# A graph network's prologue: y split on two engines beside the table chain, item tables sent first

## The chip, the cores and the metric

One NeuronCore of one Trainium2 chip runs the whole program in one launch. The metric is the device time of an execution in microseconds (us). The engines are named as in the profile: PE is TensorE (PEld its weight loads), DVE is VectorE, ACT is ScalarE, POOL is GpSimd, SP is SyncE; a letter q behind a name (SPq, DVEq) is that engine's instruction queue.

## The reference

The graph has 6250 nodes and 100000 edges, sorted by destination (dst), with features of 128 floats. Two blocks follow one another.

```python
def _sage_layer(x, src, dst, Wl_i, bl_i, Wr_i):
    agg = segment_sum(x[src], dst, N_NODES)
    cnt = segment_sum(ones, dst, N_NODES)
    return agg / clip(cnt, 1.0)[:, None] @ Wl_i + bl_i + x @ Wr_i      # three layers, relu after the first two
x = layernorm(x + sage(x))
z = concatenate([x[dst], x[src], edge_attr])                            # the convolution
msg = sigmoid(z @ Wf.T + bf) * softplus(z @ Ws.T + bs)
agg = batchnorm(segment_sum(msg, dst, N_NODES))
x = layernorm(x + relu(layernorm(agg + x)) + x)
```

## The kernel before, in words

**Data.** Nodes are cut into 49 windows of 128 rows (NW), windows into 7 chunks of 7 (NCH, CW); edges into 784 tiles of 128 (NT). A layer first makes y = h @ Wl and keeps it in DRAM (`y_dram`), and the residual h @ Wr in SBUF (`res`). For layer 0 these are `first_y` (L780) and `first_res` (L790) on PE, `first_copy` (L1198) and `first_res_copy` (L1204) on ACT. SP stores y chunk by chunk (L453).

**Two ways of summing.** 256 tiles (KT) whose destinations span fewer than 12 rows are summed densely: DVE builds two one-hots for a tile (`build`, L1909), PE multiplies them to counts (`count`, L895), ACT evicts them (`evict`, L1261), and for each of 26 groups of 10 tiles PE multiplies the counts with y (`multiply`, L914, 49 matmuls). For this product y stands in SBUF split into three bf16 parts (`y_parts`), whose sum is y to float accuracy: cast to bf16, subtract, cast the rest, subtract, cast. The other 528 tiles are gathered: POOL fetches 128 rows of y for each with an indirect DMA (L724), four tiles are a quad, 132 quads in a layer, in a ring of 12 (RQ). An item is a product of a quad with one window's one-hot: DVE builds the one-hot (`onehots`, L1898), PE multiplies (`item`, L905), DVE adds to `acc` (`add_item`, L1958). 182 items a layer make 26 turns of 7 (IT); 17 of them are woven with the counting, the last 9 with the adding of dense groups by pairs. SP feeds POOL: it sends the indices of a quad into `idx` when the slot's last item has been summed (`quad`, L532), ten quads ahead (AHEAD).

**Tables.** Which quad, window and column an item has is computed on the chip. DVE works out the schedule in a long chain of small instructions, from L1659 on: tiles are ranked and permuted (perms, L1686, with PE's products L831 to L841), then `schedule` and `part_of` make the item tables (to L1799), and a second call of `schedule` (L1800) the convolution's. PE transposes them (L861, L868), DVE copies them out (L1828, L1832), SP carries them through DRAM into one row of SBUF, `q_regs` and `regs` (L499 to L508). The engines read them there with `reg_load`: 7 words at an address of `it * 7` for each turn's list on PE (L887, L888) and DVE (L1906, L1954), and 12 on SP (L521).

**Order around the change.** All of it is written out by hand, with semaphores between the engines. DVE waits for `order_ready`, which SP raises at L493 after all stores of y have landed, before it starts the chain. ACT copies all seven residual chunks, waits for `q_regs` (L1208), then reads y back from DRAM two chunks at a time (`read_y`, L1241). DVE clears `acc` (L1835), waits for both tables (L1836), writes constants (L1839), and starts on the layer (`sage_adds`, L2040). Layer 0's first pair of turns is `counting_turns(0, first=True)`: before the additions of items 0 to 4 it splits chunks 0; 1, 2; 3, 4; 5; 6 (`SPLITS_AT`, `split_y`, L1927). In layers 1 and 2 the same split is done in their first turns.

```python
SPLITS_AT = [[0], [1, 2], [3, 4], [5], [6]]
...
                        if first and at < len(SPLITS_AT):
                            for c in SPLITS_AT[at]:
                                split_y(0, c)
                        add_item(0, it, i, sums, columns)
```

Of the kernel before, what the change touches and what calls it, by code (L numbers as in the profile page):

```python
# [5 lines left out]
P = 128  # L6
N = 6250
E = 100000
F = 128
# [12 lines left out]
CW = 7  # L22
# [29 lines left out]
NIC = 2  # L52
OH_SLOTS = [0, 1, 2, 3, 0, 1, 2]
# [18 lines left out]
SPLITS_AT = [[0], [1, 2], [3, 4], [5], [6]]  # L72
# [11 lines left out]
assert NW == CW * NCH and EP == P * NT  # L84


def build_gnn(nc, x, xT, src, dst, srcT, ea, eaT, w0, bl, blT, w1, we, b1, bn, out):
# [11 lines left out]
    with ctx:  # L99
# [20 lines left out]
        regs_dram = dram("regs_dram", (3 * NC, P), i32)  # L120
        q_regs_dram = dram("q_regs_dram", (6 * NIC, P), i32)
# [18 lines left out]
        q_regs = sb("q_regs", [1, 6 * NIC * P], i32)  # L140
# [46 lines left out]
        y_again = [work[:, EA_AT + k * CW * F:EA_AT + (k + 1) * CW * F].rearrange("p (u f) -> p u f", f=F) for k in range(2)]  # L187
        iota_c = dlo[:, 0:CELLS // 2].bitcast(bf16)
# [115 lines left out]
        tabT = work[0:3 * NC, 9344:9344 + P].bitcast(i32)  # L304
        q_tabT = work[0:6 * NIC, 9472:9472 + P].bitcast(i32)
# [13 lines left out]
        tabf = sb("tabf", [P, 3, NC])  # L319
        q_tabf = sb("q_tabf", [P, 6, NIC])  # L320
# [20 lines left out]
        def ps_first(h):  # L341
# [15 lines left out]
            chosen permuted y_in y_split cells counted counts_put multiplied reduced dense_sent nat_in order_ready idx_given ea_sorted rows rowsf rows_tr dlo_ready  # L357
# [51 lines left out]
        P_BANKS = (0, 1, 6, 7)  # L409

# [22 lines left out]
        def _(sp):  # L433
# [67 lines left out]
            sp.dma_start(q_regs[:, :], q_regs_dram.rearrange("r p -> (r p)").rearrange("(o k) -> o k", o=1))\  # L501
                .then_inc(s["tab_back"], 16)
            sp.wait_ge(s["tabT"], 2)
            sp.wait_ge(s["tab_back"], 32)
            sp.dma_start(regs_dram, tabT).then_inc(s["tab_back"], 16)
            sp.wait_ge(s["tab_back"], 48)
            sp.dma_start(regs[:, :], regs_dram.rearrange("r p -> (r p)").rearrange("(o k) -> o k", o=1))\
# [12 lines left out]
            def load_items(first, a, b):  # L520
                sp.reg_load(l_regs[a:b], q_regs[0:1, bass.ds(first, b - a)])  # L521
# [8 lines left out]
            def sage_quads(layer):  # L530

                def quad(it, q, done):  # L532
                    ahead = q + AHEAD
                    if isinstance(it, int) and it * RQ + ahead >= QG:
# [10 lines left out]
                def turn(it):  # L545
                    n = RQ if not isinstance(it, int) or it == 0 else RQ - AHEAD
                    first = it * RQ + (4 * NIC * P + AHEAD - RQ)
                    if isinstance(it, int) and it == 0:
                        done = [None] * (RQ - AHEAD) + load_items(4 * NIC * P, RQ - AHEAD, RQ)
                    else:  # L550
                        done = load_items(first, 0, n) + [None] * (RQ - n)
# [29 lines left out]
            with sp.Fori(0, NCH) as it:  # L581
# [3 lines left out]
                sp.wait_ge(s["x1_sent"], (it + 1) * 16)  # L585
# [7 lines left out]
            sp.wait_ge(s["tab_back"], 64)  # L593
            sp.wait_ge(s["tab_back"], 32)
# [37 lines left out]
            def needed(m):  # L632
                sp.reg_load(n_regs, q_regs[0:1, bass.ds(m * RC + (5 * NIC * P - RC), RC)])
# [136 lines left out]
        def _(pe):  # L770
# [51 lines left out]
            te.matmul(ps[0:ROWS, 7, 8:9], lhsT=tri[0:ROWS, 0:ROWS], rhs=t_cum[:, CH - 1:CH], start=True, stop=True).then_inc(s["permuted"], 1)  # L822

# [20 lines left out]
            first_res(0)  # L844
# [16 lines left out]
            te.transpose(ps[0:6 * NIC, 5, 0:P], q_tabf[:, :, :].rearrange("p r c -> p (r c)"), ident[:, :])\  # L861
                .then_inc(s["tables_put"], 1)
            for c in range(NIC):
# [4 lines left out]
            te.transpose(ps[0:3 * NC, 5, P:2 * P], tabf[:, :, :].rearrange("p r c -> p (r c)"), ident[:, :])\  # L868
                .then_inc(s["tables_put"], 1)
            pe.wait_ge(s["loads"], LOADS * 16)  # L870
            pe.wait_ge(s["ones_col"], 2)
            pe.wait_ge(s["tab_back"], 32)
# [6 lines left out]
            def sage_sums(layer):  # L879
# [6 lines left out]
                def load_turn(it):  # L886
                    pe.reg_load(t_regs, q_regs[0:1, bass.ds(it * IT, IT)])  # L887
# [1503 lines left out]
```

## Time and profile before

| | |
|---|---|
| three runs | 3545.97, 3549.5, 3554.33 us; median 3549.5 |
| the profiled execution | 3549.38 us, span 3547.6 us |
| busy, share of the span | PE 75%, DVE 61%, ACT 34%, POOL 65% |
| granted TensorE clock over the span | 0.895 of full |
| layer 0, first and last addition of an item (L1962) | 126.1 us and 869.5 us |
| first and last gather of layer 0 (L724) | 63.56 us and 863.33 us |

The busy shares are means over the whole program. The change touches the first 190 us, so the rows below are mostly of that stretch. In a list of instructions the brackets at the end of a row hold the idle time of its engine ahead of it and what ended it. The granted clock is a share of 2.4 GHz.

### The profile page before, as it was taken

Reading aid. Unit: us, or ns where it says so; the run is one execution under the profiler, and the core shown is the slowest. Engines: PE = TensorE matmul, PEld = TensorE weight load, DVE = VectorE, ACT = ScalarE, POOL = GpSimd, SP = SyncE. Lnnn points to the kernel's source line nnn. Section 1 sums busy time; section 2 is a strip of 40 time slices with the busy share of each in tenths; the row PEclk is TensorE's granted clock in tenths of the full one; section 3 lists DMA queues with packets and bytes.
Section 4 is the critical chain, followed back from the end, with each engine's and each line's share of the span. In section 5 each row is a group of like instructions: output and inputs, shape, how many; then the busy total and the mean of one; then the engine's idle time right before and its main releaser. Section 6 shows DMA issues by size and latency. Waiting matters only on the chain. (4 is left out here: it accounts for less than half of the span.)

```text
span 3547.6 us, 70629 instructions
## 1 busy us (share of the span) xinstructions
PE 2659.6 (75%) x16221; PEld 1996.7 (56%) x16222; DVE 2168.2 (61%) x4954; ACT 1192.1 (34%) x1646; POOL 2317.7 (65%) x2399
## 2 busy tenths in 40 slices
PE   5368888666697776566888765578888888888874
PEld 5145555465465555464555554556666666666653
DVE  5834544355732224457554544568888888888886
ACT  1023332200100000010000000158888888888865
POOL 2357777576677777756777777537777777777620
PEclk8589999887799998777989987899999999999997
DMA  4254444322565553226877752254444444444421
GB/s 122 77 169 145 139 131 143 112 50 59 153 172 156 146 149 97 53 66 184 245 222 241 221 137 63 56 159 126 127 127 126 128 126 127 126 116 119 114 58 37
DMA packets 345773, 454.44 MB, mean 128 GB/s; under 512 B 135431, under 2 KB 260386, under 8 KB 342099
## 3 DMA queue, kind: packets, MB, share of 16 engines
q0 software_dynamic: 88624, 207.58, 21.7%
q10 hardware_dynamic: 101984, 181.27, 15.9%
q1 hardware_dynamic: 155092, 64.77, 7.0%
q8 instruction: 27, 0.44, 0.1%
q14 instruction: 46, 0.38, 0.0%
HBM read 357.03 MB, written 101.90 MB: 129 GB/s over the span
## 5 line engine op out<-in xcount | busy, mean ns | idle before, releaser
L724 POOL DMA_INDIRECT shared<-y_dram,idx x1584 | 1523.1, 962 | 681.2 <-issue 506.4
L910 PE MATMUL ps<-shared,work 128*128 x4368 | 680.7, 306 | 384.3 <-issue 220.6
L764 POOL DMA_INDIRECT shared<-q_dram,idx x784 | 777.5, 992 | 284.0 <-issue 204.6
L910 PEld LDWEIGHTS ps<-shared,work 128*128 128x128 f32 x4368 | 619.5, 216 | 452.4 <-issue 440.2
L1962 DVE TENSOR_TENSOR acc<-acc,ps 128x129 f32 x546 | 156.4, 286 | 891.7 <-PE ps L910 736.6
L1114 PE MATMUL ps<-pq,work 128*128 x1664 | 497.0, 401 | 150.3 <-issue 87.6
L2251 DVE TENSOR_TENSOR work<-ps,shared 128x256 f32<-128x256 f32 x832 | 294.8, 416 | 175.6 <-PE ps L1117 156.4
L1114 PEld LDWEIGHTS ps<-pq,work 128*128 128x128 f32 x1664 | 256.6, 195 | 244.5 <-issue 173.4
L929 PE MATMUL ps<-pq,work 128*128 128x385 bf16 x1456 | 296.2, 354 | 84.4 <-DVE work L1950 34.4
L1386 ACT ACTIVATE pq<-ps,blT_sb 128x512 f32<-128x512 f32 (+1 forms) x28 | 16.5, 632 | 888.2 <-PE ps L1013 888.2
L1265 ACT CAST work<-ps 128x600 bf16<-128x600 f32 x260 | 159.8, 661 | 413.3 <-PE ps L902 344.9
L1900 DVE SCALAR_TENSOR_TENSOR work<-ps,w_of,dstT_sb 128x512 f32<-128x512 f32 x370 | 275.2, 745 | 1.2 <-issue 1.2
L1467 ACT ACTIVATE work<-work 128x1024 f32<-128x1024 f32 x208 | 219.8, 1057 | 125.8 <-DVE work L2251 125.7
L929 PEld LDWEIGHTS ps<-pq,work 128*128 128x128 bf16 x1456 | 149.9, 104 | 186.5 <-issue 79.7
L2260 DVE SCALAR_TENSOR_TENSOR work<-work,ps 128x1024 f32<-128x1024 f32 x208 | 251.5, 1209 | 1.3 <-ACT ps L1477 1.3
L1133 PE MATMUL ps<-work 128*128 128x128 f32 x1664 | 242.0, 289 | 0.8 <-DVE work L2272 0.8
L1409 ACT ACTIVATE rs<-ve 128x7 f32<-128x7 f32 x21 | 4.4, 210 | 691.6 <-DVE ve L2165 691.0
L1117 PE MATMUL ps<-we_rows,ea_sb 128*128 128x256 bf16 x832 | 230.4, 277 | 0.0
L1133 PEld LDWEIGHTS ps<-work 128*128 128x128 f32 x1664 | 202.2, 192 | 48.2 <-issue 48.2
L1473 ACT ACTIVATE work<-work 128x1024 f32<-128x1024 f32 x208 | 216.6, 1041 | 0.0
L1477 ACT ACTIVATE ps<-work 128x1024 f32<-128x1024 f32 x208 | 213.9, 1028 | 6.6
L929 PE MATMUL ps<-shared,work 128*128 128x385 bf16 x1092 | 204.3, 336 | 2.3 <-DVE shared L1933 2.3
(359 smaller groups left out, 3627.8 us busy)
## 6 DMA issues: line engine op xcount, KB each, us to landing
work<-counts_dram ACTq DMA_DIRECT2D x156, 384.0 KB
counts_dram<-work ACTq DMA_DIRECT2D x26, 1568.0 KB
shared<-y_dram,idx POOLq DMA_INDIRECT x1584
ea_parts<-work ACTq DMA_DIRECT2D x128, 196.0 KB
ea_sb<-ea_parts SPq DMA_DIRECT2D x196, 128.0 KB
work<-counts_dram ACTq DMA_DIRECT2D x52, 416.0 KB
shared<-q_dram,idx POOLq DMA_INDIRECT x784
y_dram<-work SPq DMA_DIRECT2D x21, 448.0 KB, 3.1
```

Of the source, the lines that this page charges most:

```text
L724: pool.indirect_dma_start(msg[:, u, 0:F], None, y_dram, bass.IndirectOffsetOnAxis(ap=idx[:, u:u + 1], axis=0)).then_inc(s_quad[q], 16)
L764: pool.indirect_dma_start(q_ring[:, u * 2 * F:(u + 1) * 2 * F], None, q_dram, bass.IndirectOffsetOnAxis(ap=idx[:, u:u + 1], axis=0)).then_ ...
L910: last = te.matmul(ps[:, SUM_BANKS[i], 0:FA], lhsT=oh4[:, OH_SLOTS[i], u, :], rhs=shared[:, bass.ds(place + u * FA, FA)], start=u == 0, st ...
L929: last = te.matmul(ps[:, DENSE_BANK, 0:YB - 1], lhsT=counts[:, w, :], rhs=y_parts(w, 1)[:, 0, 0:YB - 1], start=w == 0, stop=w == NW - 1)
L1114: te.matmul(o, lhsT=ohT[:, (slot - 1) % 2, t, :], rhs=pq[:, bass.ds(w_of_pair[t] * (2 * F), 2 * F)], start=True, stop=False)
L1117: last = te.matmul(o, lhsT=ea_sb[:, bass.ds(e_of_pair[t] * P, P)], rhs=we_rows[:, :], start=False, stop=True)
L1133: te.matmul(ps_flat[:, bass.ds(blocks[t] * P + AGG_BANK * 512, P)], lhsT=oh[:, (slot - 3) % GB, t, :], rhs=mm[:, (slot - 3) % 2, t, :], st ...
L1467: sc.activation(log_, pre[:, slot % 2, :, :], ACT.Abs).then_inc(s["absd"], 1)
L1473: sc.activation(log_, log_, ACT.Exp, scale=-1.0).then_inc(s["expd"], 1)
L1900: v.scalar_tensor_tensor(out=oh4[:, slot, :, :], in0=(iota_ps if layer else iota[:, :]).unsqueeze(1).to_broadcast([P, QT, P]), scalar=w_of ...
L2251: last = v.tensor_tensor(pre[:, slot % 2, t, :], ps_pre[:, slot % 2, t, :], q_ring[:, bass.ds(slots[t] * (2 * F), 2 * F)], ALU.add)
L2260: v.scalar_tensor_tensor(out=gates, in0=pre_, scalar=0.0, in1=ps_log, op0=ALU.max, op1=ALU.add)\
```

## The change

1. DVE's chain waits for the loads of dst and src (`nat_in`) itself; `order_ready` is gone.
2. PE does the residual products 0 to 2 right after its first triangular product, ahead of the permutations; ACT copies these three, then reads y.
3. Y is split with ACT and DVE together. ACT reads four chunks at once into four buffers (`y_first`), casts, DVE subtracts (`less_part`), twice; then chunks 4 to 6. ACT's queue is: four reads, four casts, residual copies 3 to 6, the clearing of `acc`, four second casts, four third casts with the next three reads between them, nine casts. DVE subtracts chunks 0 to 3 between the item tables and the convolution's schedule, chunks 4 to 6 after it, and then waits for `y_split` to reach 7.
4. The item tables are signalled, transposed and copied out before the convolution's schedule is computed. One of their six rows, the convolution's, moves to the other table.
5. `q_regs` is laid out anew: each turn's seven words stand in eight, written by eight DMAs; a read of seven words becomes one of four and one of three, each at a multiple of four; SP's of twelve become three of four. This holds for all layers.
6. SP sends 12 quads of indices up front instead of 10.

```diff
+Q_TABLES = [(NEEDED_AT, 0, 0, TURNS, IT, WIDE), (PLACES_AT, 1, 0, TURNS_ALL, IT, WIDE), ...
+y_first = [work[:, at_:at_ + CW * F]... for at_ in (EA_AT, EA_AT + CW * F, 6328, 6328 + CW * F)]
 # SP
-            sp.sem_inc(s["order_ready"], 1)
-            for q in range(AHEAD):
+            for q in range(RQ):
                 sp.dma_start(idx[:, q * QT:(q + 1) * QT], src_c[:, q * QT:(q + 1) * QT]).then_inc(s_idx[q], 16)
-            sp.dma_start(q_regs[:, :], q_regs_dram...)
+            for at_, row_, first_, turns_, n_, wide_ in Q_TABLES:
+                sp.dma_start(q_regs[0:1, at_:at_ + turns_ * wide_]..., from_dram).then_inc(s["tab_back"], 16)
 # PE
             te.matmul(ps[0:ROWS, 7, 8:9], lhsT=tri[0:ROWS, 0:ROWS], ...).then_inc(s["permuted"], 1)
+            for it in range(3):
+                first_res(it)
...
-            first_res(0)
...
-            first_res(1)
-            for it in range(2, NCH):
+            for it in range(3, NCH):
                 first_res(it)
...
                 def load_turn(it):
-                    pe.reg_load(t_regs, q_regs[0:1, bass.ds(it * IT, IT)])
-                    pe.reg_load(g_regs, q_regs[0:1, bass.ds(it * IT + NIC * P, IT)])
+                    for k in range(0, IT, 4):
+                        pe.reg_load(t_regs[k:k + 4], q_regs[0:1, bass.ds(it * WIDE + (NEEDED_AT + k), min(4, IT - k))])
+                        pe.reg_load(g_regs[k:k + 4], q_regs[0:1, bass.ds(it * WIDE + (PLACES_AT + k), min(4, IT - k))])
 # ACT
-            for it in range(NCH):
+            for it in range(3):
                 first_res_copy(it)
-            act.wait_ge(s["tab_back"], 32)
+            def read_first(c):
+                act.dma_start(y_first[c % 4], y_dram[...]).then_inc(s[Y_FIRST[c % 4]], 16)
+            def cast_first(c, k):
+                if k == 0:
+                    act.wait_ge(s[Y_FIRST[c % 4]], (c // 4 + 1) * 16)
+                else:
+                    act.wait_ge(s["y_made"], subs_before(c, k))
+                sc.copy(y_parts(c * CW, CW)[:, :, k * F:(k + 1) * F], y_first[c % 4]).then_inc(s["y_cast"] if k < 2 else s["y_split"], 1)
+            act.wait_ge(s["permuted"], 4)
+            for it in (NCH - 2, NCH - 1):
+                act.wait_ge(s[Y_SENT[it % 2]], (it // 2 + 1) * 16)
+            for c in range(4):
+                read_first(c)
+            for c in range(4):
+                cast_first(c, 0)
+            for it in range(3, NCH):
+                first_res_copy(it)
+            sc.copy(acc[:, :], zero[:, :].to_broadcast([P, NW * FA])).then_inc(s["acc_clear"], 1)
+            for c in range(4):
+                cast_first(c, 1)
+            act.wait_ge(s["permuted"], 7)
+            for c in range(4):
+                cast_first(c, 2)
+                if c + 4 < NCH:
+                    act.wait_ge(s["y_split"], c + 1)
+                    read_first(c + 4)
+            for k in range(3):
+                for c in range(4, NCH):
+                    cast_first(c, k)
+            act.wait_ge(s["tab_back"], TAB_Q)
 # DVE
-            dve.wait_ge(s["order_ready"], 1)
+            dve.wait_ge(s["nat_in"], 32)
...
+            alone(dve)
+            dve.sem_inc(s["tab"], 1)
+            dve.wait_ge(s["tables_put"], 2)
+            v.tensor_copy(q_tabT, ps[0:5 * NIC, 5, 0:P]).then_inc(s["tabT"], 1)
+            dve.wait_ge(s["tables_put"], 3)
+            link(v.tensor_copy(w_of[:, :], ps[:, 6, 0:NIC * P]))
+            def less_part(c, k):
+                dve.wait_ge(s["y_cast"], casts_before(c, k))
+                v.tensor_tensor(y_first[c % 4], y_first[c % 4], y_parts(c * CW, CW)[:, :, k * F:(k + 1) * F], ALU.subtract).then_inc(s["y_made"], 1)
+            for k in range(2):
+                for c in range(4):
+                    less_part(c, k)
             schedule(7, NC, kcol, S_)
...
-            dve.wait_ge(s["r0"], NCH)
-            v.memset(acc[:, :], 0.0).then_inc(s["acc_clear"], 1)
-            dve.wait_ge(s["tab_back"], 64)
+            for k in range(2):
+                for c in range(4, NCH):
+                    less_part(c, k)
+            dve.wait_ge(s["y_split"], NCH)
+            dve.wait_ge(s["tab_back"], TAB_Q + 16)
...
-                        if first and at < len(SPLITS_AT):
-                            for c in SPLITS_AT[at]:
-                                split_y(0, c)
                         add_item(0, it, i, sums, columns)
```

## Rows read from the trace of the kernel before

**Rows 1.** Stretches: length, busy us of each engine, granted clock, DMA share, GB/s
```profile
120.00:166.00 46.00, 11.82 (x54) 8.81 (x53) 45.04 (x63) 6.10 (x10) 3.96 (x4) 0.54 0.28 92
189.00:411.00 222.00, 181.67 (x1145) 118.56 (x1143) 99.88 (x329) 65.16 (x106) 154.75 (x160) 0.93 0.50 161
411.00:671.00 260.00, 228.78 (x1443) 150.65 (x1444) 127.63 (x422) 83.62 (x136) 183.15 (x188) 0.96 0.44 138
```

**Rows 2.** Groups of DVE, 113 to 166.2 us: busy us, mean ns | idle before
```profile
L1933 DVE CAST pq<-work 128x896 bf16<-128x896 f32 x12 | 12.9, 1079 | 0.3
L1933 DVE CAST shared<-work 128x896 bf16<-128x896 f32 x9 | 9.8, 1084 | 0.2
L1936 DVE TENSOR_TENSOR work<-work,pq 128x896 f32<-128x896 f32 x8 | 8.7, 1092 | 0.3
L1936 DVE TENSOR_TENSOR work<-work,shared 128x896 f32<-128x896 f32 x6 | 6.5, 1092 | 0.2
```

**Rows 3.** Waits, 125 to 190 us: us in total, times, longest
```profile
POOL shared L724 <- DMA idx<-ea_sb: 64.4, 1, 64.4
```

**Rows 4.** Instructions in time, all engines: start us, us, what, idle before
```profile
51.54 5.85 PE L831 MATMUL ps<-pq,shared 112*128 112x264 f32 x16 [6.58 <-DVE pq L1688]
...
60.99 6.39 SPq L496 DMA_DIRECT2D idx<-ea_sb  x10
...
69.59 2.83 PE L841 MATMUL ps<-work,shared 112*128 112x264 f32 x12
...
102.86 1.06 PE L864 MATMUL ps<-work,ones 128*128 128x128 f32 x4
...
123.95 0.94 POOL L724 DMA_INDIRECT shared<-y_dram,idx  x1 [0.30 <-issue]
...
186.82 21.63 SPq L540 DMA_DIRECT2D idx<-ea_sb  x6
...
189.26 0.94 POOL L724 DMA_INDIRECT shared<-y_dram,idx  x1 [64.38 <-DMA idx<-ea_sb]
```

**Rows 5.** Instructions of DVE in time
```profile
26.57 0.21 DVE L1595 COPY work<-ps 128x50 f32<-128x50 f32 x1 [1.98 <-PE ps L804]
...
39.24 0.63 DVE L1659 CAST shared<-shared 112x896 f32<-112x896 int32 x1 [12.47 <-SPq L492]
...
95.89 0.48 DVE L1799 TENSOR_SCALAR work<-ident,work 128x128 f32<-128x128 f32 x2
...
105.01 0.17 DVE L1824 COPY conv_w<-work 128x7 f32<-128x7 f32 x1
...
113.37 0.21 DVE L1839 TENSOR_SCALAR dlo<-iota 128x44 bf16<-128x44 f32 x1 [0.16 <-DMA regs<-regs_dram]
...
186.87 0.29 DVE L1962 TENSOR_TENSOR acc<-acc,ps 128x129 f32 x1 [1.60 <-PE ps L910]
...
294.53 0.29 DVE L1962 TENSOR_TENSOR acc<-acc,ps 128x129 f32 x1 [2.23 <-PE ps L910]
...
319.35 0.29 DVE L1962 TENSOR_TENSOR acc<-acc,ps 128x129 f32 x1 [0.23 <-PE ps L910]
```

**Rows 6.** DMA issues, 0 to 70 us: KB each, median us to landing
```profile
shared<-in_src SPq DMA_DIRECT2D x1, 392.0 KB, 10.0
```

**Rows 7.** Table reads by line (ns min/median/max; last row: 114 to 115 us)
```profile
L887 PEldq TENSOR_LOAD <-q_regs x78: 1061/1702/2653, 109.3 to 2252.8; - x78
L1906 DVEq TENSOR_LOAD <-q_regs x84: 528/1626/3966, 114.5 to 2255.3; - x84
L1859 DVEq TENSOR_LOAD <-regs x208: 337/342/357, 2353.3 to 3425.2; - x104
L1906 DVEq TENSOR_LOAD <-q_regs x1: 768/768/768, 114.5 to 114.5; - x1
```

**Rows 8.** Groups of ACT: busy us, mean ns | idle before
```profile
L1206 ACT COPY pq<-ps 128x896 f32<-128x896 f32 x7 | 6.3, 906 | 49.6 <-PE ps L797 49.6
```

**Rows 9.** DMA issues, 108 to 120 us
```profile
work<-y_dram ACTq DMA_DIRECT2D x2, 448.0 KB, 4.1
```

More of the change, by code:

```diff
@@ L52 @@
 NIC = 2
+WIDE = 8
 OH_SLOTS = [0, 1, 2, 3, 0, 1, 2]
@@ L71 @@
 COUNTS_LAST = [2, 3, 3, 2, 4, 3, 3]
-SPLITS_AT = [[0], [1, 2], [3, 4], [5], [6]]
 FIRST_SLOTS = 6
@@ L187, in build_gnn @@
         y_again = [work[:, EA_AT + k * CW * F:EA_AT + (k + 1) * CW * F].rearrange("p (u f) -> p u f", f=F) for k in range(2)]
+        y_first = [work[:, at_:at_ + CW * F].rearrange("p (u f) -> p u f", f=F) for at_ in (EA_AT, EA_AT + CW * F, 6328, 6328 + CW * F)]
         iota_c = dlo[:, 0:CELLS // 2].bitcast(bf16)
@@ L520, in load_items @@
             def load_items(first, a, b):
-                sp.reg_load(l_regs[a:b], q_regs[0:1, bass.ds(first, b - a)])
+                for k in range(a - a % 4, b, 4):
+                    lo, hi = max(a, k), min(b, k + 4)
+                    sp.reg_load(l_regs[lo:hi], q_regs[0:1, bass.ds(first + lo, hi - lo)])
                 for q in range(a, b):
@@ L533, in quad @@
                     ahead = q + AHEAD
-                    if isinstance(it, int) and it * RQ + ahead >= QG:
+                    if isinstance(it, int) and (it * RQ + ahead >= QG or layer == 0 and it == 0 and ahead < RQ):
                         pass
@@ L632, in needed @@
             def needed(m):
-                sp.reg_load(n_regs, q_regs[0:1, bass.ds(m * RC + (5 * NIC * P - RC), RC)])
+                for k in range(0, RC, 4):
+                    sp.reg_load(n_regs[k:k + 4], q_regs[0:1, bass.ds(m * WIDE + (CONV_DONE_AT - WIDE + k), min(4, RC - k))])
                 for q in range(RC):
@@ L933, in load_pairs @@
                 def load_pairs(turn):
-                    pe.reg_load(d_regs, q_regs[0:1, bass.ds(turn * IT + (NIC * P + NI1), IT)])
+                    for k in range(0, IT, 4):
+                        pe.reg_load(d_regs[k:k + 4], q_regs[0:1, bass.ds(turn * WIDE + (PLACES_AT + TURNS * WIDE + k), min(4, IT - k))])
                     return [pe.snap(r, min_val=0, max_val=(NGR - PT) * FA) for r in d_regs]
@@ L1248, in read_y @@
                         .then_inc(s["y_in"], 16)
-                for it in (NCH - 2, NCH - 1):
-                    act.wait_ge(s[Y_SENT[it % 2]], (it // 2 + 1) * 16 if layer == 0 else y_sent(layer - 1, it))
-                if layer == 0:
-                    act.wait_ge(s["permuted"], 4)
-                elif layer == 1:
-                    act.wait_ge(s["rowsf"], 1)
-                for c in range(2):
-                    read_y(c)
-                if layer == 0:
-                    act.wait_ge(s["y_split"], 1)
+                if layer:
+                    for it in (NCH - 2, NCH - 1):
+                        act.wait_ge(s[Y_SENT[it % 2]], y_sent(layer - 1, it))
+                    if layer == 1:
+                        act.wait_ge(s["rowsf"], 1)
+                    for c in range(2):
+                        read_y(c)
                 def evict(n, k, row):
@@ L1905, in load_columns @@
             def load_columns(first, n):
-                dve.reg_load(c_regs[0:n], q_regs[0:1, bass.ds(first, n)])
+                for k in range(0, n, 4):
+                    dve.reg_load(c_regs[k:min(k + 4, n)], q_regs[0:1, bass.ds(first + k, min(4, n - k))])
                 return [dve.snap(r, min_val=0, max_val=(QL - 1) * QT) for r in c_regs[0:n]]
@@ L1927, in split_y @@
             def split_y(layer, c):
-                dve.wait_ge(s["y_in"], (layer * NCH + c + 1) * 16)
-                if c == 0 and not layer:
-                    v.memset(counts[:, :, GT * SPAN:P], 0.0)
+                dve.wait_ge(s["y_in"], Y_IN0 + ((layer - 1) * NCH + c + 1) * 16)
                 y_, p_ = y_again[c % 2], y_parts(c * CW, CW)
@@ L1980, in load_pairs @@
             def load_pairs(turn):
-                dve.reg_load(b_regs, q_regs[0:1, bass.ds(turn * IT + (3 * NIC * P + NI1), IT)])
-                dve.reg_load(f_regs, q_regs[0:1, bass.ds(turn * IT + (2 * NIC * P + NI1 + LOOK), IT)])
+                for k in range(0, IT, 4):
+                    dve.reg_load(b_regs[k:k + 4], q_regs[0:1, bass.ds(turn * WIDE + (SUMS_AT + TURNS * WIDE + k), min(4, IT - k))])
+                    dve.reg_load(f_regs[k:k + 4], q_regs[0:1, bass.ds(turn * WIDE + (PAIR_COLS_AT + k), min(4, IT - k))])
                 return ([dve.snap(r, min_val=0, max_val=(NW - 1) * FA) for r in b_regs],
```

112 lines of the change are left out of this document (69 added, 43 removed).

## The prediction

> **What bounds the kernel now.** The page's first section comes first: PE, DVE and GpSimd (POOL) are each busy for well over half of the span and none for nearly all of it. The shares name no single bound, so the stage that the change touches is read alone. Next the stretches: from 120 to 166 us DVE works 45.04 of 46 us while PE has 11.82 and POOL 3.96; from 189 us on it is the other way round, PE 181.67 of 222 us, POOL 154.75, DVE 99.88 [rows 1]. DVE bounds 46 us and little afterwards. The groups of that stretch say what it does: 21 casts and 14 subtractions of 128x896, the split of y into three bf16 parts, 12.9 + 9.8 + 8.7 + 6.5 = 37.9 us [rows 2]. They stand between the first additions of items. The waits say who pays: POOL has one wait of 64.4 us for an index transfer [rows 3], from the gather at 123.95 to the one at 189.26. SyncE issues that transfer only at 186.82 [rows 4], since its slot is free only when enough items have been summed, and items are summed as fast as DVE takes them. The eighth addition is at 186.87 [rows 5]. Everything after hangs on it: a gather starts 1.25 us after the one before (0.94 and 0.30 of issue, [rows 4]), so the layer's other 480 gathers alone are 600 us, and the counting that PE does beside them starts there too. I carry the sum out for the moment of the eighth addition.
>
> **1. The order is not awaited behind y's stores.** DVE ends L1595 at 26.78 and starts L1659 at 39.24, a wait of 12.47 us for SyncE's L492 [rows 5]. What L1659 needs are dst and src in rows; src is issued third on SyncE's queue, in the first 5 us, and landed 10.0 us later [rows 6], by 15. The gain is between 0 (reading the flag and jumping over the fallback costs DVE as much as the wait did) and 12.5. For the flag and the jump, which the wait covered, I leave 2.2 us: an estimate between one and two table reads of 0.77 to 1.63 [rows 7]. So 10.2. PE's last y product ends at about 32, DVE's first step comes at about 34, and three residual products behind it, under 2 us each with ACT's 0.906 copies between them [rows 8], end near 40 (an estimate), before the permutations come at 51.54 - 10.2 = 41.3 [rows 4]. The permutation matmuls began at the lower rate (16 in 5.85 us, 0.366 each; of the later, same-shaped ones 12 in 2.83, 0.236 [rows 4]); with PE busy just before them up to 2 us could come back. I count nothing.
>
> **2. The item tables ahead of the convolution's.** DVE ends L1799 at 96.37 [rows 5]; shifted 86.2, and 0.3 for two chained writes: signal at 86.5. PE's transpose and the four passes of L864 take until about 1.5 us after the signal (end 103.92 [rows 4]); two copies more, 88.6. SyncE then issues eight small transfers where it had one. Ten index transfers took 6.39 us to issue [rows 4]; eight such are over before 96, with nothing queued behind them but the convolution's tables, which DVE finishes at 106; PE waits for them, but has no item before DVE's one-hots. So they cost nothing, and up to 5 us if that cover went.
>
> **3. The split beside the chain.** ACT may read y once the last permutation matmul is over, 72.42 [rows 4] - 10.2 = 62.2. A 448 KB read took 4.1 us [rows 9]; four one after another land by 79 at worst. ACT's copy of 896 columns costs 0.906 [rows 8]: the four first casts are done at 80, the four residual copies at 85.5 (in step with PE's products, and before 86.5, when PE is wanted for the tables), and the clearing of acc, 6321 columns at the same rate, at 92. For ACT's casts out of SBUF, which no row shows, the bounds are 0.9 [rows 8] and twice that; I take 1.0, beside DVE's 1.08 [rows 2]. DVE subtracts chunks 0 to 3 twice, 8 x 1.09 [rows 2] = 8.7 us, 88.6 to 97.4, with ACT one chunk behind it. The convolution's schedule took from 96.3 to 105.2 [rows 5], 8.9 us: 106.3. A transpose and a copy, 1.1: 107.4. ACT's third casts and the reads of chunks 4 to 6 start near 97 and land by 109.5; three casts, six subtractions (6.5 us) and the last two casts end at 116. Fourteen subtractions remain on DVE, the 21 casts and the clear do not.
>
> So DVE begins the constants of L1839 at 116 instead of 113.37 [rows 5], 2.6 us late: it has swapped a wait and a clear for 15.2 us of subtractions. What is gone is what came after. Before, the builds ahead of item 0 were over at 120.5, just where the first cast began; now at 123.5 with a memset. From there on there are only builds and additions: seven items and one dense product took 294.53 to 319.35, 24.8 us [rows 5]. The clock granted was 0.54 from 120 to 166, nearly the lower of the levels 1.2 and 2.4 GHz, with PE mostly idle, and 0.93 from 189 to 411 [rows 1]; the new turn begins low, and as in L831 some 16 matmuls pay, 16 x (0.366 - 0.236) = 2 us. Eighth addition: 123.5 + 24.8 + 2 = 150, against 186.87: **37 us**.
>
> The index transfer and POOL's restart follow it as before, 152 for 189. The first 48 gathers also start and end 10 us earlier, worth nothing; so are the two index transfers that SyncE sends up front in addition (12 for 10), on an idle queue.
>
> **4. Table reads in fours.** Each read of seven words becomes one of four and one of three. Seven words took 1.63 (DVE) and 1.70 us (PE) in the median and 1.06 at PE's lowest, three words 0.768, four aligned words in the convolution 0.342 [rows 7]. The lows come when the start is a multiple of four, every fourth turn: four words travel together there, the rest singly. So the new pair costs 0.34 + 0.77 + 0.1 of address = 1.2 us; three turns in four it gains 0.4 to 0.5, in the fourth it loses 0.15. PE has two reads a turn, 17 turns in layer 0's counting part: at most 10 us if PE were the bound throughout. From 189 to 411 POOL is nearly always at work (154.75 busy of 222, where 0.94 of 1.25 would be 167); from 411 to 671 it gives way (183.15 of a possible 195) and PE has 228.78 of 260 [rows 1]. Nine turns, two reads, 0.25: 4; I take 2. In layers 1 and 2 POOL's gathers bound: 0. Both ends: 10 gained, 3 lost (an instruction more for each read and none faster).
>
> The Trainium skill speaks against this part: "Runtime: NRT & Kernel Launch", section "Instruction fetch mechanics", gives such a load some 200 ns for each register, even in bulk. By that rule seven words cost the same whole or split, the term is 0, and the sum 3512. The seven-word median agrees (0.23 a word); the four words in 0.342 do not.
>
> **Sum.** The profiled execution took 3549.38 us, its span 3547.6. 3549.4 - 37 - 2 = **3510**. The three runs' median is 3549.5 (3545.97 to 3554.33), so it holds for that too.
>
> **Rivals.**
> (a) *The start is late or cold.* If ACT's casts out of SBUF cost double, DVE is ready some 8 us later, and if PE stays at the lower rate for the whole first turn, its 24.8 us grow by up to half. For it: 0.54 granted there [rows 1]. Against: the rate rose within one group of matmuls in L831. Time 3520 to 3530.
> (b) *More than the sum.* The full 12.5 us of part 1, 2 of the permutations, 8 more of the table reads: 3498 to 3501. For it: PE at 0.88 of 411 to 671 [rows 1]. Against: POOL's ring caps it.
> (c) *The gathers take it back.* If POOL's own stream ended layer 0 from its first gather on, only that gather's start would count, and a stop between layers could swallow the 10 us: 3540 to 3549. Against: the 64.4 us [rows 3] are a hole in that very stream, and it closes with the eighth item.
> (d) *Slower: y's reads choke the table chain.* ACT takes reads, casts and residual copies in order; the copies free PE for the item tables, which DVE awaits. Seven reads of r us move the start by about 7 (r - 4.1). From r = 9.4 on the kernel loses; at three times the row, 12.3, it takes 3510 + 57 = 3567. For it: four reads stand at once beside the gathers, which is new. Against: the two of the row ran beside gathers too, at 4.1 [rows 9].
>
> **How the numbers follow.** No change can be told from one within 0.2%, 7 us. Chances: forecast (3502 to 3519) 0.66, (a) 0.15, (b) 0.10, (c) 0.05, of which most is within 0.2%, (d) 0.04. The range goes down to (b)'s 3498 and up to (a)'s 3530; (c), (d) and the tails of (a) and (b) are left out, some 0.15. Faster 0.92, same 0.04, slower 0.04.
>
> **What would show it.** The chain of L1659 starts near 29, with no wait of 12 us. The subtractions stand in two groups, near 89 to 97 without gaps and near 108 to 115. The constants of L1839 come at 114 to 118. DVE has no cast of 128x896 in layer 0. The eighth item is added near 150, and POOL's longest wait for an index in layer 0 is near 40 us (112 to 152), not 64. Three-word reads take 0.77 and four-word reads 0.34. The layer's last addition moves as much as the eighth. I am wrong if the eighth item comes early and the last does not, or if ACT's residual copies behind the reads end after 87 and hold the tables up.

## The result, and the profile after

The changed kernel takes 3501.2 us (median of 4 runs, 3492.5 to 3502.4) where the kernel before took 3548.6: ratio 0.9859, 95% interval 0.9845 to 0.9872, 47 us less by the medians and 50 by the ratio. The profiled execution spans 3500.4 us against 3547.6. The forecast was 3510 in a range of 3498 to 3530.

The marks of layer 0, the first additions after and before (L2037 is L1962 of before): eighth item, item 113 (the first of turn 16), last of the layer.

DVE in time, after; columns: start us, us, engine line op out<-in, count, [idle before <- what ended it]:
```profile
148.85 0.29 DVE L2037 TENSOR_TENSOR acc<-acc,ps 128x129 f32 x1 [1.54 <-PE ps L946]
...
592.02 0.29 DVE L2037 TENSOR_TENSOR acc<-acc,ps 128x129 f32 x1 [2.54 <-PE ps L946]
...
823.36 0.29 DVE L2037 TENSOR_TENSOR acc<-acc,ps 128x129 f32 x1 [6.19 <-PE ps L946]
```
The same two later marks before:
```profile
640.64 0.29 DVE L1962 TENSOR_TENSOR acc<-acc,ps 128x129 f32 x1 [1.74 <-PE ps L910]
...
869.48 0.29 DVE L1962 TENSOR_TENSOR acc<-acc,ps 128x129 f32 x1 [4.35 <-PE ps L910]
```
The eighth addition moved from 186.87 [rows 5] to 148.85, by 38.0 us. From there to turn 16 (I call it the woven stage: 15 turns with counting) it was 453.8 us and is 443.2, 10.6 less. The last nine turns give 2.5 back (228.8 to 231.3). At the layer's end the gain is 46.1, at the ends of layers 1 and 2 it is 48.8 and 49.2: some 3 more are won in the two together.

The stretches of after that answer to [rows 1], each begun at nearly the same work:
```profile
118.00:152.00 34.00, 27.68 (x168) 20.47 (x169) 20.30 (x66) 11.80 (x20) 7.26 (x8) 0.83 0.17 62
152.00:374.00 222.00, 183.24 (x1157) 118.18 (x1156) 102.63 (x340) 66.54 (x109) 158.41 (x162) 0.95 0.50 162
374.00:622.00 248.00, 222.02 (x1417) 142.97 (x1417) 123.77 (x409) 81.25 (x133) 182.61 (x187) 0.99 0.45 144
```
The stretch in which DVE worked 45 of 46 us is gone: in its place PE works 27.7 of 34 us at a granted clock of 0.83 where it had 0.54. The last stretch does nearly the same matmuls and gathers (1417 and 187, before 1443 and 188) in 248 us instead of 260.

The chain of DVE, after (compare [rows 5]):
```profile
26.42 0.21 DVE L1661 COPY work<-ps 128x50 f32<-128x50 f32 x1 [1.99 <-PE ps L840]
32.18 0.63 DVE L1726 CAST shared<-shared 112x896 f32<-112x896 int32 x1 [5.55 <-issue]
32.72 0.62 DVE L1727 TENSOR_SCALAR shared<-shared 112x896 int32<-112x896 int32 x1
34.89 0.63 DVE L1728 TENSOR_SCALAR shared<-shared 112x896 int32<-112x896 int32 x1 [1.54 <-issue]
...
91.31 8.10 DVE L1876 TENSOR_TENSOR work<-work,pq 128x896 f32<-128x896 f32 x8
...
107.95 0.17 DVE L1903 COPY conv_w<-work 128x7 f32<-128x7 f32 x1
108.78 0.28 DVE L1907 CAST work<-ps 23x128 int32<-23x128 f32 x1 [0.66 <-PE ps L904]
108.98 6.08 DVE L1876 TENSOR_TENSOR work<-work,shared 128x896 f32<-128x896 f32 x6
116.07 0.19 DVE L1914 TENSOR_SCALAR dlo<-iota 128x44 bf16<-128x44 f32 x1 [1.00 <-ACT shared L1259]
```
The wait of 12.47 us for SyncE has gone, and a stop of 5.55 us that no other engine ends has come, with a second of 1.54. The subtractions stand in two groups, one before and one behind the convolution's schedule, and the constants (L1839 before, L1914 now) begin at 116.07, released by ACT's last cast.

ACT beside it:
```profile
65.27 3.26 ACTq L1251 DMA_DIRECT2D work<-y_dram  x4
69.09 0.94 ACT L1259 CAST pq<-work 128x896 bf16<-128x896 f32 x1 [21.46 <-DMA work<-y_dram]
70.80 0.94 ACT L1259 CAST pq<-work 128x896 bf16<-128x896 f32 x1 [0.77 <-DMA work<-y_dram]
...
82.91 0.91 ACT L1243 COPY pq<-ps 128x896 f32<-128x896 f32 x1 [0.66 <-PE ps L833]
83.71 5.46 ACT L1271 COPY acc<-zero 128x6321 f32<-128x6321 f32 x1
```
POOL's restart, 64.38 us of wait before [rows 4]:
```profile
151.33 1.40 POOL L760 DMA_INDIRECT shared<-y_dram,idx  x1 [24.91 <-DMA idx<-ea_sb]
```
The wait is shorter by more than the start moved, since the first 48 gathers start 7.1 us earlier (56.46 for 63.56) but end 1.5 later (126.42 for 124.89).

The table reads (ns, least/median/most), four-word and three-word ones together on a line:
```profile
L923 PEldq TENSOR_LOAD <-q_regs x156: 333/700/978, 108.9 to 2204.4; - x156
L1982 DVEq TENSOR_LOAD <-q_regs x162: 344/742/2329, 117.4 to 2205.5; - x162
```

### The profile page after: what moved, and what is told of

The parts are those of the page before. It is cut to its first block, busy times and chain, and to the rows that moved or that the text cites. A ratio compares the mean times of both kernels' runs of the same rounds, so it can differ in the third digit from the quotient of the medians.

```text
span 3500.4 us, 71571 instructions
## 1 busy us (share of the span) xinstructions
PE 2665.2 (76%) x16221; PEld 2000.1 (57%) x16222; DVE 2142.4 (61%) x4932; ACT 1216.7 (35%) x1668; POOL 2333.4 (67%) x2399
## 4 chain that ended last, share of the span: by engine, by line
POOL 35%; PE 21%; issue 19%; DVE 10%; DMA 9%; DVEq 3%; SPq 2%; ACT 2%; POOLq 0%; ACTq 0%
POOL shared L760 28%; POOL shared L800 8%; DMA shared<-q_dram,idx 6%; PE ps L955 6%; PE ps L946 4%; PE ps L1151 3%; PE ps L938 2%; SPq L638 1%; DVE work L2326 1%; PE ps L965 1%; DVE work L2010 1%; PE ps L1154 1%; DMA counts_dram<-work 1%; DVE work L2335 1%; ACT work L1481 1%
## 5 line engine op out<-in xcount | busy, mean ns | idle before, releaser
L760 POOL DMA_INDIRECT shared<-y_dram,idx x1584 | 1538.5, 971 | 623.3 <-issue 498.9
L2037 DVE TENSOR_TENSOR acc<-acc,ps 128x129 f32 x546 | 156.3, 286 | 901.8 <-PE ps L946 770.9
L2326 DVE TENSOR_TENSOR work<-ps,shared 128x256 f32<-128x256 f32 x832 | 294.6, 416 | 177.6 <-PE ps L1154 149.4
L1452 ACT ACTIVATE pq<-ps,blT_sb 128x512 f32<-128x512 f32 (+1 forms) x28 | 16.5, 631 | 887.6 <-PE ps L1050 887.6
```

The lines of the kernel that those rows point to most:

```text
L760: pool.indirect_dma_start(msg[:, u, 0:F], None, y_dram, bass.IndirectOffsetOnAxis(ap=idx[:, u:u + 1], axis=0)).then_inc(s_quad[q], 16)
L2326: last = v.tensor_tensor(pre[:, slot % 2, t, :], ps_pre[:, slot % 2, t, :], q_ring[:, bass.ds(slots[t] * (2 * F), 2 * F)], ALU.add)
```

## The experiments

"Stage" is the time from the eighth addition to turn 16. The marks are of the profiled execution, the total is the median of all; the ratio is to the kernel before, run beside it on the same chip. Its medians there were 3548.6 to 3553.2, so two totals of this table compare to a few us only.

| kernel | eighth | stage | layer 0 ends | total | ratio, 95% interval | name |
|---|---|---|---|---|---|---|
| before | 186.9 | 453.8 | 869.5 | 3548.6 | 1 | |
| after | 148.9 | 443.2 | 823.4 | 3501.2 | 0.9859 (0.9845 to 0.9872) | |
| before + reads | 190.0 | 442.0 | 862.9 | 3539.8 | 0.9972 (0.9962 to 0.9981) | e1 |
| after, reads whole | 150.2 | 451.4 | 832.7 | 3511.1 | 0.9897 (0.9882 to 0.9912) | e2 |
| before + order | 182.0 | 454.0 | 865.6 | 3544.2 | 0.9989 (0.9980 to 0.9998) | e3 |
| after, order awaited | 153.9 | 445.3 | 830.5 | 3503.3 | 0.9872 (0.9857 to 0.9887) | e4 |
| split only (and PE's products ahead) | 153.3 | 451.4 | 836.3 | 3519.7 | 0.9916 (0.9899 to 0.9932) | e5 |
| after, tables late | 148.8 | 444.1 | 824.1 | 3500.1 | 0.9865 (0.9848 to 0.9881) | e6 |
| after again (PE) | 149.5 | 444.1 | 825.9 | 3500.0 | 0.9857 (0.9840 to 0.9873) | e10 |
| after again (DVE) | 148.0 | 443.6 | 823.4 | 3502.8 | 0.9868 (0.9852 to 0.9885) | e11 |
| after, PE's reads slow | 149.2 | 459.7 | 840.0 | 3521.4 | 0.9911 (0.9898 to 0.9925) | e12 |
| after, DVE's reads slow | 149.4 | 455.3 | 835.4 | 3509.3 | 0.9872 (0.9857 to 0.9887) | e13 |
| after, reads of eight | 147.3 | 419.4 | 795.3 | 3470.6 | 0.9772 (0.9759 to 0.9785) | e7 |
| the same + early steps | 138.8 | 420.2 | 788.2 | 3465.2 | 0.9749 (0.9735 to 0.9762) | e9 |

### The reads, done alone and undone (e1, e2)

To the kernel before, the new tables and reads alone; from the kernel after, the reads alone taken away:
```diff
-                    pe.reg_load(t_regs, q_regs[0:1, bass.ds(it * IT, IT)])
+                    for k in range(0, IT, 4):
+                        pe.reg_load(t_regs[k:k + 4], q_regs[0:1, bass.ds(it * WIDE + (NEEDED_AT + k), min(4, IT - k))])
...
```


> The kernel before with the table reads alone changed: item tables laid at multiples of eight words, each read of seven as a read of four and one of three. All else, the split and the waits, as before. The stage from the eighth addition of layer 0 to the addition of turn 16 took 453.7 us before and 443.2 after. Theory R (the reads give the extra that I had sized at 2): that stage takes 444 to 446 us here, and the total falls by 8 to 10 less up to 5 for the nine small transfers in place of one before DVE's first one-hots: 3539 to 3545. Theory S (the shorter stage comes with the earlier start, by clock or phase, and the reads give the 2 of the prediction): stage 451 to 453, total 3546 to 3552. Theory W (200 ns for a word, whole or split): stage 453 to 455, total 3549 to 3554.

> The changed kernel with the table reads put back: tables seven words apart, read by one load of seven. The split, the order and the early item tables stay. Theory R: the stage from the eighth addition to that of turn 16 goes from 443.2 back to 451 to 454, total 3509 to 3512. Theory S: it stays at 443 to 446, total 3501 to 3504. The eighth addition stays within 2 us of 148.9 by either.

Alone the reads shorten the stage by 11.8 us, taken away they lengthen it by 8.2; the total moves by 9.8 and 9.9 by the medians, 10 and 13 by the ratios. So the reads are the extra, not the earlier start, and a rule that prices a word alike in any read (0 us) is out. The 200 ns for each register that the prediction quotes from the Trainium skill ("Runtime: NRT & Kernel Launch", section "Instruction fetch mechanics") are given there for the loads that the runtime puts in, which the page has read from HBM; the tables here lie in SBUF, so the page is not refuted, it speaks of another load. The first also showed what the new layout costs where nothing hides it:
```profile
119.35 0.19 DVE L1865 TENSOR_SCALAR dlo<-iota 128x44 bf16<-128x44 f32 x1 [5.67 <-DMA regs<-regs_dram]
```
Without the split beside the chain, the nine small transfers put the constants 6.0 us later (113.37 [rows 5]), and the eighth addition 3.1 later.

### The order, done alone and undone (e3, e4)

```diff
-            dve.wait_ge(s["order_ready"], 1)
+            dve.wait_ge(s["nat_in"], 32)
```


> The kernel before with one edit: DVE's chain waits for dst and src in rows, no longer for SyncE's signal behind y's stores. Prediction's term by itself: chain 10.2 us earlier, total 3539. What the changed kernel's trace showed: chain's first step 32.2 (5.4 to 7 us earlier, the rest goes into the jump over the fallback body) and 1.8 back from the permutation matmuls: the constants of L1839 at 106 instead of 113.4, eighth addition at 180, total 3541 to 3543. Rival: the split in layer 0 waits for something that does not move, or PE's first residual products are now in the permutations' way, since they are not placed ahead here: under 4 us, total above 3545.

> The changed kernel with DVE's wait for SyncE's signal behind y's stores restored; split, early tables and reads as changed. If the order's term counts in full beside the split: chain 7.2 us later at the cell steps, constants of L1914 at 123, eighth addition at 156, total 3508 to 3509. Rival: ACT's clear and casts are what DVE waited for (its constants at 116.07 were released by ACT), so ACT, whose reads of y hang on the permutations only in part, gives some back: eighth addition at 150 to 153, total 3502 to 3506.

Alone: chain at 32.07, eighth addition 4.8 us earlier, total down 5.4. I had expected 7 at the eighth addition; the 1.8 us from quicker permutation matmuls did not come here (see step 1 below). Undone:
```profile
121.15 0.19 DVE L1915 TENSOR_SCALAR dlo<-iota 128x44 bf16<-128x44 f32 x1 [1.00 <-ACT shared L1260]
```
The constants come 5.1 us later, ACT, too, since its reads follow the permutations, and the eighth addition 5.1 later: ACT gave nothing back, and the 7.2 us that I had read off the trace were too many. The total alone, 3503.3, would have fitted the rival's 3502 to 3506. The layer's end moves by 7.1. The total moved by 2.1 by the medians and 4.6 by the ratios, with intervals that overlap. The part is worth 5, not 10.2.

### The split alone, and the tables late (e5, e6)

The second of these has only this edit, the first has it beside the two undoings above:
```diff
-            dve.sem_inc(s["tab"], 1)
-            dve.wait_ge(s["tables_put"], 2)
-            v.tensor_copy(q_tabT, ps[0:5 * NIC, 5, 0:P]).then_inc(s["tabT"], 1)
...
             link(v.tensor_copy(conv_w[:, :], sch[:, J3, 0:NC]))
             alone(dve)
             dve.sem_inc(s["tab"], 1)
+            dve.sem_inc(s["tab"], 1)
+            dve.wait_ge(s["tables_put"], 2)
+            v.tensor_copy(q_tabT, ps[0:5 * NIC, 5, 0:P]).then_inc(s["tabT"], 1)
...
```


> The changed kernel with all but the split undone: DVE's chain waits for SyncE's signal behind y's stores, item tables leave DVE after the convolution's schedule, reads of seven words whole. What stays is the split beside the chain (and PE's first three residual products placed early). Forecast from the single effects seen so far: eighth addition at 148.9 + 5.1 (order) + 6 (tables late) + 1.4 (reads) = 161 against 186.9 before, stage to turn 16 of 451 to 454, total 3518 to 3524: the split alone is worth 26 to 30 us. Rival: the parts need one another (ACT's reads of y start late, DVE finds no cover for its subtractions, so that the split is spread over the stage after): eighth addition above 168, total above 3530.

> The changed kernel with part 2 undone: DVE signals the item tables together with the convolution's, after the second schedule, and copies them out then; the nine small transfers of the new layout stay. The prediction costed this part at 0, with up to 5 us if its cover went. Theory now: DVE's constants of L1914 wait for the tables' return, which takes some 13 us from the copy: constants near 121 to 122 in place of 116.1, eighth addition 5 to 6 us later (154 to 155), total 3506 to 3508. Rival (the 0 holds both ways, PE's clear and ACT's casts hide the return): eighth addition 148 to 150, total 3500 to 3503.

The split, with PE's first three residual products ahead of the permutations, brings the eighth addition 33.6 us forward and the total down by 31.1 us: two thirds of the whole. I had expected the eighth addition at 161, of which 6 us were for the late tables; the other run shows that these cost nothing. With the tables late my theory of 5 to 6 us failed and the prediction's 0 held:
```profile
106.83 0.28 DVE L1901 CAST work<-ps 10x128 int32<-10x128 f32 x1 [0.63 <-PE ps L897]
...
108.35 6.08 DVE L1869 TENSOR_TENSOR work<-work,shared 128x896 f32<-128x896 f32 x6
116.39 0.18 DVE L1912 TENSOR_SCALAR dlo<-iota 128x44 bf16<-128x44 f32 x1 [1.96 <-DMA regs_dram<-work]
```
The tables now end the wait, 1.0 us after ACT would have (1.96 of wait where ACT's was 1.00), and the constants come 0.3 us later than in the kernel after: the tables' return lies almost wholly behind the six subtractions and ACT's last cast. I had priced it from the run in which DVE had no subtractions there.

### Which engine's reads (e10 to e13)

> The changed kernel with each of TensorE's per-turn table reads issued twice (nothing else changes): 2 more pairs of a four-word and a three-word read, 2.4 us, in each turn. Theory PE (TensorE bounds the stage from the eighth addition to turn 16, so a us of read on it is a us of time): the stage goes from 443.2 to 470 to 482, total 3525 to 3545. Theory POOL (the gathers bound it and the reads' gain was at its cap): stage 443 to 455. Theory DVE (it was VectorE's reads that paid): stage 443 to 446 here, and more than 455 with VectorE's reads doubled.

> The changed kernel with each of VectorE's per-turn table reads issued twice: 2.2 to 2.4 us more of VectorE in each turn. Theory PE: VectorE is busy for 215 of 443 us in the stage, so it absorbs them: stage 443 to 447, total 3501 to 3506. Theory DVE: every item's one-hots wait behind the reads once a turn: stage 460 or more, total above 3518.

These two answered nothing: the executed program has no doubled reads (156 on PE's line as before), so a load whose registers are loaded again before use was evidently dropped on the way to the chip.
```profile
L926 PEldq TENSOR_LOAD <-q_regs x156: 333/670/982, 109.9 to 2205.6; - x156
```
They are the kernel after twice more, and show how well it repeats: stage 443.2, 444.1, 443.6; total 3501.2, 3500.0, 3502.8. So I made one engine's reads slow instead, by its tables' place:
```diff
-NEEDED_AT = 0
+NEEDED_AT = 1
...
+                    pe.reg_load(t_regs, q_regs[0:1, bass.ds(it * WIDE + NEEDED_AT, IT)])
```


> The changed kernel with TensorE's reads alone slow: one load of seven words, its tables shifted by one word so that no load starts at a multiple of four (1.70 us each where the pair of loads takes 1.1). VectorE's and SyncE's loads stay in fours. Theory PE (TensorE's reads carry the gain of the stage between the eighth addition and turn 16): stage 451 to 456 in place of 443.2, total 3509 to 3515. Theory DVE: stage 443 to 446, total 3500 to 3504. If both share it, about half in each of this and the next kernel.

> The changed kernel with VectorE's reads alone slow: one load of seven words, its tables shifted by one word (1.63 us each where the pair takes 1.1). TensorE's and SyncE's loads stay in fours. Theory PE: stage 443 to 446, total 3500 to 3504. Theory DVE: stage 451 to 456, total 3509 to 3515.

The first fence is PE's line with its tables shifted, the second DVE's:
```profile
L922 PEldq TENSOR_LOAD <-q_regs x78: 1697/1703/2158, 108.6 to 2221.0; - x78
```
```profile
L2031 DVEq TENSOR_LOAD <-q_regs x78: 1621/1634/5107, 119.4 to 2215.4; - x78
```
The stage grew by 16.5 us with PE's reads slow (459.7, more than the 456 that I had allowed) and by 12.1 with DVE's. PE reads 1.2 us longer in a turn (3.4 for 2.2), 18 us in 15 turns; DVE 1.0 longer in turns of one kind and 1.6 in the other, some 20. So neither theory is right alone: a us of read costs 0.9 us of stage on PE and 0.6 on DVE. That the two hand items to one another, so that a stop of one is not made up, is my explanation; no run takes it apart. In layers 1 and 2 the loss nearly stands still (16.7 us at the end of layer 0, 17.9 at that of layer 2, for PE): there the reads are nearly hidden, as predicted. The two runs leave out SyncE, whose reads in the stage also fell with the change, from 26.5 us in all (e2) to 10.5; no run slows them alone.

### Reads of eight, and DVE's first steps early (e9, e7)

```diff
-                    for k in range(0, IT, 4):
-                        pe.reg_load(t_regs[k:k + 4], q_regs[0:1, bass.ds(it * WIDE + (NEEDED_AT + k), min(4, IT - k))])
+                    pe.reg_load(t_regs + [pe_x], q_regs[0:1, bass.ds(it * WIDE + NEEDED_AT, WIDE)])
...
+            dve.wait_ge(s["nat_in"], 32)
+            order_steps(link)
             dve.wait_ge(s["edges_in"], 16)
```
(`order_steps` is L1726 to L1734 of the kernel after; the second kernel below has the reads alone.)

> The changed kernel with two edits more, a candidate for a faster one. (1) VectorE's first nine steps on dst and src in rows (5.3 us of work) stand in its idle 4.8 us ahead of the wait for the edge row, and once more inside the fallback body, since they need no answer from the flag: the chain behind them should start 5 us earlier (cell step at 34 in place of 39.0), the constants at 111 to 112, the eighth addition at 143 to 145. Rival: those transfers have not landed by 17, or the stop for the code after the jump only moves: under 2 us. (2) Each per-turn read of seven is one load of eight words at a multiple of eight, the eighth word unused. By the reads seen (0.33 for four at a multiple of four, 0.23 for each other word) it takes 0.56 us against 1.1 for the pair; stage to turn 16 then 433 to 440 in place of 443.2, where the gathers cap it (some 345 gathers at 1.25 us are 431). Rival: a load of eight costs 8 x 0.2 or more, 1.7 to 1.9 us: stage 452 to 456. Total by both: 3487 to 3493.

> The changed kernel with only the second edit of the candidate before: each per-turn read of seven as one load of eight words at a multiple of eight. VectorE's first steps stay where the change has them. If the two edits of the candidate are independent, the chain and the constants stay (116), the eighth addition comes at 146 (2.6 us from the reads of the first turns), the stage to turn 16 takes 420 as in the candidate, and the total is 3473 to 3477. Rival: the stage was shorter there because its start was earlier (clock, or phase of the gathers): stage 430 or more, total above 3482.

Both beat the kernel after: 3470.6 with the reads of eight, 3465.2 with the early steps too (its ratio to before, divided by that of the kernel after: 0.9888). Both totals lie below what I had expected. PE's reads in e7:
```profile
L923 PEldq TENSOR_LOAD <-q_regs x78: 587/592/1202, 109.6 to 2170.1; - x78
```
Eight words at a multiple of eight take 0.592 us. The stage is 23.8 us shorter, in e9 23.0: my 433 to 440, held up by a cap from some 345 gathers, was too careful. Only 314 gathers start in e7's stage, 392 us at 1.25. In e7 the gain on the kernel after grows on, from 28.1 us at the end of layer 0 to 33.8 at that of layer 2, so in the later layers the reads are not hidden altogether. Turns 9 and 10, first additions after and in e7:
```profile
392.26 0.27 DVE L2037 TENSOR_TENSOR acc<-acc,ps 128x129 f32 x1
...
424.14 0.29 DVE L2037 TENSOR_TENSOR acc<-acc,ps 128x129 f32 x1 [3.51 <-PE ps L946]
...
448.33 0.29 DVE L2037 TENSOR_TENSOR acc<-acc,ps 128x129 f32 x1 [0.36 <-PE ps L946]
```
```profile
377.33 0.28 DVE L2040 TENSOR_TENSOR acc<-acc,ps 128x129 f32 x1
...
407.84 0.29 DVE L2040 TENSOR_TENSOR acc<-acc,ps 128x129 f32 x1 [3.48 <-PE ps L946]
...
430.30 0.28 DVE L2040 TENSOR_TENSOR acc<-acc,ps 128x129 f32 x1
```
31.9 and 24.2 us become 30.5 and 22.5, and so through the whole stage; PE and DVE read 1.0 us less each in a turn. In e9 the early steps end just as the edge row is there, and the chain behind the jump starts 7.5 us earlier (39.02 to 31.54), since the second stop (1.54) has gone with the 5.3 us of steps:
```profile
22.11 0.17 DVE L1664 TENSOR_TENSOR_SCAN shared<-shared 112x7 f32<-112x7 f32 x1
22.32 0.57 DVE L1669 CAST pq<-work 128x784 f32<-128x784 int32 x1
...
31.54 0.63 DVE L1749 CAST shared<-shared 112x896 f32<-112x896 int32 x1 [5.06 <-issue]
```
This start is not kept whole: e9 is ahead of e7 by 8.5 us at the eighth addition, by 7.1, 3.3 and 0.8 at the ends of the three layers, and by 5.4 in the median total, with intervals that touch. What takes it back in layers 1 and 2 was not looked into.

## Why the prediction was right, and where it was not

**What bounds, and the moment that decides: right, the size by luck in part.** The eighth addition moved by 38.0 where I had 37, and everything after hung on it. But the 37 were 10.2 for the order and 26.8 for the rest, and the runs give the order some 5 (e3, e4) and the split with PE's products ahead 33.6 (e5): two errors of 5 to 7 us cancelled. The layer's last addition moved by 8 more, not by the same: that is step 4.

**Step 1, the order: 10.2 forecast, 5.1 found** (e3, e4). The wait of 12.47 us covered more than the 2.2 us that I left for the flag and the jump: the stop behind L1661 is 5.55 us, and 1.54 follow two instructions later. 12.47 less these two is 5.4, which is what the chain gained. DVE's queue in the first stop (ns least/median/most, then first and last start in us):
```profile
L1663 DVEq TENSOR_LOAD <-flag x1: 1068/1068/1068, 26.7 to 26.7; - x1
...
L1665 DVEq COMPARE_BRANCH  x1: 67/67/67, 28.1 to 28.1; - x1
```
Reading the flag is done by 28.1, and 4.0 us pass between the branch and L1726 at 32.18. The Trainium skill has the rule that I did not apply here ("Runtime: NRT & Kernel Launch", section "Instruction fetch mechanics"): a taken branch out of the prefetched window stalls its engine until the target is fetched. The trace agrees with that, an idle engine behind a jump over a long body with nothing to wait for; the page gives no price. Packets of the instruction queues fall into both stops (one on q8 and one on q14 from 28.2 to 32.1 us, one on q14 from 32.7 to 34.8) and none from 13 to 26, but the trace does not say for which engine, so the fetch as the cause is likely and not shown. The part that I counted as nothing came: with residual products just ahead, the first 16 permutation matmuls ran at the rate of the later ones (0.233 us each),
```profile
39.38 7.25 PE L833 MATMUL ps<-w_sb,acc 128*128 128x128 f32 x42
46.47 3.73 PE L869 MATMUL ps<-pq,shared 112*128 112x264 f32 x16
```
3.73 us where 5.85 stood [rows 4], so that DVE was 7.2 us ahead behind them (L1757 at 52.90, before at 60.09). That it is the products placed ahead is seen in e3, which has none of them there, where the same 16 matmuls took 6.30 us:
```profile
45.99 6.30 PE L830 MATMUL ps<-pq,shared 112*128 112x264 f32 x16 [6.58 <-DVE pq L1688]
```
and in e4, which has them there behind the old wait, and where they took 3.73 again.

**Step 2, the tables first: right, 0** (e6). The transfers put the constants 6 us later where nothing covers them (e1); the cover is the subtractions and ACT's casts.

**Step 3, the split: right, with two errors that cancelled.** Constants at 116 forecast, 116.07 found, although the chain was 3 us later than I had it. The second half was quicker by as much: ACT's reads landed 1.7 us apart (casts at 69.09 and 70.80), not 4.1, and its cast out of SBUF took 0.94, as I took it (1.0), not twice that; the second group of subtractions starts right after the schedule. From the constants on 8.1 us to the first addition and 24.7 for seven items, against 7.5 and 26.8: the 2 us that I allowed for a low clock in the first turn were not paid (granted 0.83).

**Step 4, the table reads: the mis-sized term, 2 forecast, 8 to 12 found in the stage, some 10 in the total** (e1, e2). The duration of the new pair was right (1.2 forecast; 2.2 us for two pairs in a turn, where 3.4 stood). What failed is the weighing of who pays. I let PE's reads count in nine turns alone, because POOL was nearly always at work before 411, and left DVE's out. But POOL was not at a cap: with reads of eight the stage fell to 419.4 us, in which POOL was busy for 309. And DVE's reads cost, too, 0.6 of a us for each where PE's cost 0.9 (e13 and e12). A time share of 0.7 on POOL was no bound; the items' way through PE and DVE in turn was nearer to it.

**Rivals.** (b) named the right surplus in part (8 more of the reads, 2 of the permutations), by the wrong counterweight (POOL's ring), and its full 12.5 us of step 1 did not come. The measured 3501.2 lies just below the 3502 to 3519 that I gave to the forecast, at (b)'s edge. (a), (c) and (d) are out: the first turn ran at 0.83, the gain of the start stood at every layer's end, and y's reads landed 1.7 us apart. (In (d) the kernel would lose from 9.7 us for a read, not 9.4, for the 2 us of step 4 count too.) The result lies where the forecast's own 3510 less the 8 that step 4 lacked puts it, 3502.

**A sign that did not come.** POOL's longest wait for an index was 24.9 us, not near 40: the first 48 gathers lasted 8.6 us longer than before, most of it beside the subtractions (last section). Nothing hung on it, since POOL restarts behind the eighth addition.

**Open.** In the kernel after with whole reads (e2) the turns of the longer kind took no longer than after (31.0 to 32.4 us for 31.7 to 32.5), though PE read 0.6 and DVE 0.3 to 1.6 us more in them, while in e12 and e13 they did; the slopes of the single engines (16.5 and 12.1) do not add up to the 8.2 of all reads. So which engine's reads earned the gain of the change is not settled, only that both PE's and DVE's can cost. And the time from layer 2's end to the program's end varied by itself between 1265 and 1274 us over these kernels, which is why I read effects below 5 us from the marks of layer 0, not from totals.

## What to carry to other kernels

When work is moved into the idle time of another chain, find the one event that later stages count from, and price the move at that event. Do not price a wait's removal at its full length: ask what else the wait covered, the jump and the code behind it too. Price a scalar stop (a table read) on every engine of a hand-over loop, not on the busiest one alone, and lay tables so that a turn's words start at a multiple of their group.

## What the hardware showed unexpectedly

**Table reads by place.** 0.592 us for eight words at a multiple of eight, 0.33 for four at a multiple of four, 0.75 to 0.77 for three, 1.70 for seven off such a place: two groups of four cost less than a read of three words.

**Gathers slow down beside subtractions.** A gather took 0.94 us on POOL, but 1.70 while DVE subtracted from 91.31 to 99.41, and one 6.41 in the second group:
```profile
91.25 0.94 POOL L760 DMA_INDIRECT shared<-y_dram,idx  x1 [0.30 <-issue]
92.50 1.72 POOL L760 DMA_INDIRECT shared<-y_dram,idx  x1 [0.30 <-issue]
...
98.53 1.70 POOL L760 DMA_INDIRECT shared<-y_dram,idx  x1 [0.30 <-issue]
100.53 0.94 POOL L760 DMA_INDIRECT shared<-y_dram,idx  x1 [0.30 <-issue]
...
109.47 6.41 POOL L760 DMA_INDIRECT shared<-y_dram,idx  x1 [0.30 <-issue]
```
In its first 190 us the kernel before has one slow gather of this kind, beside a long instruction with two SBUF inputs:
```profile
76.92 1.61 DVE L1726 TENSOR_TENSOR shared<-shared,w 128x1400 f32<-128x1400 f32 x1
...
77.30 2.05 POOL L724 DMA_INDIRECT shared<-y_dram,idx  x1 [0.30 <-issue]
```
With the order awaited again the subtractions started 5.07 us later and the slow gathers 5.08 (97.58, 114.55 the long one), so the two go together. The Trainium skill ("SBUF — State Buffer", section "Who interferes with whom") has DVE's instructions with two SBUF inputs contend with GpSimd's reads, and infers that the making of descriptors is spared; these rows agree with the contention, and so does layer 2: beside DVE's long instructions with one input in PSUM (L1949, L1954, L1971) all 84 gathers took 0.94 to 0.95. They bear on the inference only in part, since a gather also reads its indices from SBUF, and which of the two was held up is not shown. It cost nothing here: POOL had 24.9 us to wait anyway.
